# A two-layer decoder on one core: the first expert layer starts on full tiles of four sequences, and the rest of its routing runs beside them

## The reference

```
x = x + L0_attn(layernorm(x));  x = x + L0_xattn(layernorm(x), ctx, ctx, mask)
x = x + L0_ffn(layernorm(x))
x = x + L1_attn(layernorm(x));  x = x + L1_xattn(layernorm(x), ctx)
x = x + L1_ffn(layernorm(x))

def L0_ffn(x):                                   # 8 experts, 2 of them for each row
    probs = softmax(x @ router_w + router_b)
    topk_p, topk_i = top_k(probs, 2);  topk_p = topk_p / sum(topk_p)
    for e in range(8):
        w = sum(where(topk_i == e, topk_p, 0))
        out += w * (relu(x @ w1[e] + b1[e]) @ w2[e] + b2[e])
```

## Time and profile before

| what | us |
|---|---|
| device time, median of 3 runs | 2476.54 |
| the same, lowest and highest run | 2468.53 and 2481.51 |
| the profiled execution, its own time | 2488.47 |
| its span, first to last instruction | 2486.7 |

### The profile page before, as it was taken

The page is one execution under the profiler, slowest core; times in us unless marked ns, Lnnn a source line. Parts: engine busy times, 40 slices in busy tenths (PEclk is TensorE's granted clock), DMA queues, the critical chain, the costliest instruction groups (busy, mean ns, idle before and its releaser), DMA issues. The chain is left out here.

```text
span 2486.7 us, 41779 instructions
## 1 busy us (share of the span) xinstructions
PE 2199.1 (88%) x13780; PEld 1754.8 (71%) x13781; DVE 1184.5 (48%) x3431; ACT 962.1 (39%) x1878; POOL 640.5 (26%) x820
## 2 busy tenths in 40 slices
PE   6997887838999668888888969988999999999998
PEld 4664454527999545555555547778999999999998
DVE  4543788743333356666676535535422222222245
ACT  2221554413444324444444422330155555555411
POOL 1112667756000313333332211113600000000053
PEclk9997989859999768989999889989999999999999
DMA  9920000112222133333333110025401111111033
GB/s 318 386 97 1 1 1 33 51 71 81 70 70 72 61 83 82 82 73 71 77 86 70 35 54 4 4 84 189 143 29 34 34 35 34 34 34 34 26 102 104
DMA packets 150997, 183.31 MB, mean 74 GB/s; under 512 B 25491, under 2 KB 119251, under 8 KB 150739
## 3 DMA queue, kind: packets, MB, share of 16 engines
q1 hardware_dynamic: 136962, 146.51, 20.6%
q0 software_dynamic: 12288, 33.57, 4.3%
q10 hardware_dynamic: 1616, 1.57, 0.2%
HBM read 73.34 MB, written 74.19 MB: 59 GB/s over the span
## 5 line engine op out<-in xcount | busy, mean ns | idle before, releaser
L2257 ACT ACTIVATE a_prob<-a_st_ps 128x512 f32<-128x512 f32 (+1 forms) x384 | 197.7, 522 | 297.3 <-PE a_st_ps L2135 295.1
L2333 DVE CUSTOM_DVE_ANT_0 a_s_ps<-a_s_ps,a_causal 128x512 f32<-128x512 f32 (+3 forms) x512 | 241.2, 515 | 120.5 <-PE a_s_ps L2118 119.4
L1774 PE MATMUL e_up_ps<-e_xT,e_ring 128*128 128x128 f32 x2272 | 276.8, 275 | 0.0
L1774 PEld LDWEIGHTS e_up_ps<-e_xT,e_ring 128*128 128x128 f32 x2272 | 270.7, 192 | 3.6
L1726 POOL DMA_INDIRECT e_wgu<-slots_y,slot x64 | 61.1, 954 | 617.4 <-DMA slots_y<-e_y 572.7
L1804 ACT ACTIVATE e_ring<-e_wgu 128x512 f32 (+2 forms) x355 | 180.9, 531 | 76.1 <-PE e_up_ps L1774 74.4
L2118 PE MATMUL a_s_ps<-a_ks,rf_qs 68*128 68x512 f32 (+3 forms) x512 | 157.3, 375 | 58.1 <-DVE a_most L2333 44.8
L1809 ACT ACTIVATE e_hT<-e_up_ps 128x512 f32<-128x512 f32 x103 | 61.5, 597 | 369.7 <-PE e_y_ps L1784 362.3
L2135 PE MATMUL a_st_ps<-rf_qs,a_ks 128*128 128x512 f32 (+3 forms) x512 | 188.0, 418 | 13.6 <-DMA rf_qs<-a_m_lo 10.3
L2045 POOL TENSOR_SCALAR_AFFINE_SELECT a_prob<-a_prob 128x256 f32<-128x256 f32 x256 | 101.0, 419 | 369.8 <-ACT a_prob L2257 369.6
L1784 PE MATMUL e_y_ps<-e_wd,e_hT 128*128 x852 | 195.7, 380 | 0.0
(11 more groups left out here) (420 smaller groups left out, 4028.3 us busy)
## 6 DMA issues: line engine op xcount, KB each, us to landing
slots_x<-zero_row SPq DMA_DIRECT2D x4, 8448.0 KB, 50.2
e_xin<-slots_x SPq DMA_DIRECT2D x142, 128.0 KB, 2.0
slots_y<-e_y SPq DMA_DIRECT2D x142, 128.0 KB, 1.7
e_w<-in_L_ffn_w SPq DMA_DIRECT2D x16, 512.0 KB, 10.1
rf_qs<-a_hi SPq DMA_DIRECT2D x32, 256.0 KB, 5.0
a_ks<-a_hi SPq DMA_DIRECT2D x32, 256.0 KB, 5.1
rf_qs<-a_lo SPq DMA_DIRECT2D x32, 256.0 KB, 6.1
a_ks<-a_lo SPq DMA_DIRECT2D x32, 256.0 KB, 7.1
```

Of the source, the lines that this page charges most:

```text
L1774: last = pe.matmul(up_ps[:, j, bank, (first + n) * P:(first + n + 1) * P], weights, xT[:, j, k * P:(k + 1) * P], start=k == 0, stop=k == K ...
L2257: act.activation(prob[:, gr % 2, u // 3, (u % 3) * BANK:(u % 3) * BANK + cols], st_ps[:, u % 2, 0:cols], ACT.Exp).then_inc(exp_done, 1)
L2333: last = dve.tensor_tensor_reduce(s_ps[:, u % 2, off:off + cols], s_ps[:, u % 2, off:off + cols], causal[:, S - cols:], 1.0, -3.0e38, ALU. ...
```

## The change

The routing's state (rows, norm, `StreamedChoice`, semaphores) is held by a class `Routing` that lives through both stages. Cross attention ends after STEPS = (B + 1) * TB = 36 steps, with groups 0 to 2 placed and the 32 scatters of groups 0 and 1 issued, and with the logits of sequence 6 and the statistics of sequence 7 made. From the counts after groups 0 and 1 `order_first` takes 24 tiles that are full, level by level over the experts, and `words` writes the rows and words of these alone.

The expert stage has its first 28 tiles written out. Inside them stand the scatters of groups 2 to 4 (POOL, 32), the rows, transposes and logits of sequence 7, choice, count and `slots` of groups 3 and 4, the order of the other 47 tiles (`order_rest`, `place_rest`, `turn_order`, `words`), and the copy of the places. `late.gpsimd` follows POOL's scatters, `late.sync` stands at tile 9, `late.sync_slopes` at tile 23, `late.vector` at tile 20. y is stored back to the tile's own place in slots_x, and L1 attention gathers from there; `pack` is gone. DVE's order per tile becomes x, y, h; h goes straight into hT, where Relu works in place. The buffers of `late` and w_of now lie in a spare area. The core of the diff:

```
+FIRST_TILES = 24
+FIRST_WORDS = FIRST_TILES // UNROLL
...
+    def tiles_of(self, dve, tiles, over):
         self.link(dve, dve.tensor_tensor(tiles, self.base[:, :], self.first[:, :], ALU.subtract))
...
+        if over:
+            self.link(dve, dve.tensor_scalar(tiles, tiles, float(over), None, ALU.add))
+        self.link(dve, dve.tensor_copy(self.tiles_i[:, :], tiles))
+        self.link(dve, dve.tensor_scalar(self.tiles_i[:, :], self.tiles_i[:, :], P.bit_length() - 1, None, ALU.logical_shift_right))
+        self.link(dve, dve.tensor_copy(tiles, self.tiles_i[:, :]))
+    def levels(self, dve, tiles):
+        shape = [P, EXPERT_TILES, E]
+        self.link(dve, dve.tensor_tensor(self.by_level[:, :, :], tiles.unsqueeze(1).broadcast_to(shape),
+                                         self.level[:, :].unsqueeze(2).broadcast_to(shape), ALU.min))
+        self.link(dve, dve.tensor_reduce(self.reach[:, :], self.by_level[:, :, :], AX.X, ALU.add))
+    def find(self, dve, tiles, place):
+        self.link(dve, dve.tensor_scalar(self.within[:, :], self.reach[:, :], place, None, ALU.is_le))
+        self.link(dve, dve.tensor_reduce(self.depth[:, :], self.within[:, :], AX.X, ALU.add))
+        self.link(dve, dve.tensor_tensor(self.within[:, :], self.within[:, :], self.reach[:, :], ALU.mult))
+        self.link(dve, dve.tensor_reduce(self.begun[:, :], self.within[:, :], AX.X, ALU.max))
+        self.link(dve, dve.tensor_scalar(self.past[:, :], self.begun[:, :], place, -1.0, ALU.subtract, ALU.mult))
+        self.link(dve, dve.tensor_scalar(self.more[:, :], tiles, self.depth[:, 0:1], None, ALU.is_gt))
+        self.link(dve, dve.tensor_tensor_scan(self.until[:, :], self.g.ones[:, 0:E], self.more[:, :], 0.0, ALU.mult, ALU.add))
+        self.link(dve, dve.tensor_scalar(self.under[:, :], self.until[:, :], self.past[:, 0:1], None, ALU.is_le))
+    def order_first(self, dve):
+        full, gone, more = self.full[:, :], self.gone[:, :], self.more[:, :]
+        self.levels(dve, full)
+        self.find(dve, full, self.place[:, 0:1])
+        self.link(dve, dve.tensor_reduce(self.spot[:, 0:1], self.under[:, :], AX.X, ALU.add))
+        dve.scalar_tensor_tensor(out=self.spot[:, 1:2], in0=self.spot[:, 0:1], scalar=float(EXPERT_TILES), in1=self.depth[:, :],
+                                 op0=ALU.mult, op1=ALU.add).then_inc(self.ordered, 1)
+        dve.wait_ge(self.ordered, 1)
+        self.find(dve, full, float(FIRST_TILES))
+        self.link(dve, dve.tensor_tensor(more, more, self.under[:, :], ALU.mult))
+        self.link(dve, dve.tensor_scalar(gone, full, self.depth[:, 0:1], None, ALU.min))
+        self.link(dve, dve.tensor_tensor(gone, gone, more, ALU.add))
...
+    def order_rest(self, dve):
+        left, depth, spare, more = self.tiles[:, :], self.depth[:, :], self.spare[:, :], self.more[:, :]
+        self.tiles_of(dve, left, P - 1)
+        self.link(dve, dve.tensor_tensor(left, left, self.gone[:, :], ALU.subtract))
+        self.levels(dve, left)
+        self.find(dve, left, self.place[:, 0:1])
...
+    def place_rest(self, dve):
...
+    def turn_order(self, pe, part, bank):
+        pe.wait_ge(self.ordered, part + 1)
+        pe.matmul(bank[0:1, 0:P], self.spot[:, 0:1], self.g.ident[:, :], start=True, stop=True)
+        pe.matmul(bank[0:1, P:2 * P], self.spot[:, 1:2], self.g.ident[:, :], start=True, stop=True).then_inc(self.order_turned, 1)
+    def words(self, dve, part, bank):
+        at, until = ((0, FIRST_TILES), (FIRST_TILES, SLOT_TILES))[part]
+        word_at, word_until = ((0, FIRST_WORDS), (FIRST_WORDS, EXPERT_WORDS))[part]
+        dve.wait_ge(self.order_turned, part + 1)
...
+        dve.tensor_copy(self.g.tile_rows[0:1, at:until], bank[0:1, P:P + until - at]).then_inc(self.written, 1)
...
+    def keep_slots(self, dve):
         dve.wait_ge(self.placed, self.groups)
...
+        dve.tensor_copy(self.g.slot[:, :, :].rearrange("p t c -> p (t c)"), self.slot[:, :]).then_inc(self.written, 1)
...
-        STEPS = (B + 3) * TB
+        STEPS = (B + 1) * TB
...
-                ready = sum(n * TB for b, n in GROUPS if (b + n + 2) * TB + 2 < s) * 2
+                ready = sum(n * TB for b, n in GROUPS[0:2] if (b + n + 2) * TB + 2 < s) * 2
...
-            for j in range(RROWS):
-                pool.wait_ge(sorted_[j], 16 * 2 * TB * B // RROWS)
+            rnorm.gpsimd(B - 1)
+            rnorm.gpsimd_offset(B - 1)
...
+            pe.wait_ge(p_kept, NT)
+            route.turn_order(pe, 0, turn[:, 0, :])
...
                 for gr, t, n in chosen(i, 2):
+                    if i == STEPS - 2:
+                        route.tiles_of(dve, route.full[:, :], 0)
                     route.slots(dve, gr, t, n, seq_bank)
+                    if i == STEPS - 2:
+                        dve.wait_ge(g.zeroed, 16 * ZERO_PARTS)
+                        route.order_first(dve)
...
-            route.words(dve)
-            route.pack(dve)
-            dve.wait_ge(route.written, 3)
+            after(dve, rnorm.offset_done, B - 1)
+            dve.wait_ge(x_done, NT)
+            rnorm.vector_stats(B - 1)
+            keep_logits(B - 2)
+            route.words(dve, 0, turn[:, 0, :])
+            dve.wait_ge(route.written, 2)
...
+def over_tiles(eng, n, steps, first=1):
     looped = (n - UNROLL) // UNROLL
-    for i in range(UNROLL):
-        steps(i, i, 0, None)
-    with eng.Fori(1, looped) as u:
+    for i in range(first * UNROLL):
+        steps(i, i % UNROLL, i // UNROLL, None)
+    if first > 1:
+        for i in range(first * UNROLL, (first + 1) * UNROLL):
+            steps(i, i % UNROLL, i // UNROLL, None)
+        first += 1
...
+            for j in range(routing.RROWS):
+                sp.wait_ge(routing.sorted[j], 16 * 2 * TB)
             for i in range(AHEAD):
                 fetch(i, i)
-            late.sync()
-            late.sync_slopes()
...
             def steps(i, place, u, kind):
                 j = place % 2
+                if kind or 2 <= i:
+                    sp.wait_ge(y_kept, i - 1)
+                    sp.dma_start(rows_x[tile_row(i - 2)], y[:, j, :]).then_inc(y_out[j], 16)
+                if not kind and i + AHEAD == FIRST_TILES:
+                    sp.wait_ge(route.written, 4)
+                    for n in range(routing.RROWS):
+                        sp.wait_ge(routing.sorted[n], 16 * 2 * TB * B // routing.RROWS)
                 if kind or i + AHEAD < N:
                     fetch(i + AHEAD, place)
-                if kind or 2 <= i:
-                    sp.wait_ge(y_kept, i - 1)
-                    sp.dma_start(rows_y[i - 2], y[:, j, :]).then_inc(y_out[j], 16)
-            over_tiles(sp, N, steps)
+                if not kind and i == 9:
+                    sp.wait_ge(routing.l_done, B)
+                    late.sync()
+                if not kind and i == FIRST_TILES - 1:
+                    late.sync_slopes()
+            over_tiles(sp, N, steps, FIRST_WORDS)
...
+                if not kind and i in (2, 4):
+                    turn_routed(i // 2 - 1)
+                if not kind and i == 6:
+                    logit()
+                if not kind and i in (4, 11):
+                    gr = {4: 3, 11: 4}[i]
+                    route.count(pe, gr, TB, routing.before[:, :], route_bank)
+                if not kind and i == 15:
+                    route.turn_order(pe, 1, route_bank)
+            over_tiles(pe, N, steps, FIRST_WORDS)
...
-                    after(act, y_done, i - 2)
-                    act.activation(hT[:, 1 - j, :], h[:, 1 - j, :], ACT.Relu).then_inc(hT_kept, 1)
-            over_tiles(act, N, steps)
+                    act.activation(hT[:, 1 - j, :], hT[:, 1 - j, :], ACT.Relu).then_inc(hT_kept, 1)
+                if not kind and i == 0:
+                    rnorm.scalar_rows(LAST, free=[(routing.sorted[LAST % routing.RROWS], LAST // routing.RROWS * 16 * 2 * TB)], buf=LAST % routing.RROWS)
+                if not kind and i in (1, 8):
+                    gr = {1: 3, 8: 4}[i]
+                    route.exponentials(act, gr, GROUPS[gr][0] * TB, TB)
+                if not kind and i in (3, 5):
+                    keep_routed(i // 2 - 1)
...
+            for k in range(2 * TB * 4, 2 * NT):
+                t = k // 2
+                pool.wait_ge(route.placed, sum(1 for b, n in GROUPS if b * TB <= t))
+                pool.indirect_dma_start(g.slots_x, bass.IndirectOffsetOnAxis(ap=route.slot[:, k:k + 1], axis=0),
+                                        rnorm.rows[t // TB % routing.RROWS][:, t % TB, :], None).then_inc(routing.sorted[t // TB % routing.RROWS], 16)
+            for j in range(routing.RROWS):
+                pool.wait_ge(routing.sorted[j], 16 * 2 * TB * B // routing.RROWS)
             late.gpsimd(g)
...
-            late.vector()
             dve.wait_ge(biases, 32)
+            def choose(i):
+                if i in (0, 7):
+                    gr = {0: 3, 7: 4}[i]
+                    if gr == 4:
```

(34 more changed lines are left out.)

178 lines of the change are left out of this document (97 added, 81 removed).

## The result

The kernel before took 2473.69 us (median of 5 runs, 2468.53 to 2481.51), the changed one 2456.17 us (2450.13 to 2459.14). The ratio is 0.9921, with a 95% interval of 0.9902 to 0.9940: faster by 0.79%, some 19.5 us. The forecast was 2444.4 us, in a range of 2431 to 2459: the sign is right and the time lies in the range, near its upper end, but of a gain of 32 us only 18 to 20 arrived. The measured 2456 is the number that rival B had, and lies outside the 2434 to 2453 that the forecast gave itself. The changed kernel was measured again on two other chips, at 1.0019 (0.9995 to 1.0044) and 1.0016 (0.9993 to 1.0039) of the kernel before. There it gains nothing that these intervals show.

What follows compares the result with a forecast made beforehand. Before the experts the routing chain, no busy engine, sets the time; in the expert stage PE bounds. 45.2 - 6.0 - 4 - 1 - 1 - 0.9 = 32 us saved, so the median 2476.5 becomes 2444.4 us, range 2431 to 2459.

Steps and rivals of the forecast that it cites:

- rival B: Expert stage: DVE's blocks and POOL's work beside them hurt PE, costs together 25 of 45 us, total 2456; chance 0.17.
- The hole: Cross attention to first expert transpose: that transpose moves from 566.6 to 521.4, saving 45.2 us, with 1 us for the boundary.
- rival C: Boundary before the expert stage: 5.6 us of POOL's pause stay, total 2450 us; chance 0.11.
- PE's products: Expert stage: moved-in transposes 1.2, logits 2.1, counts 2.4 and turn_order 0.3 add 6.0 us on full PE.
- DVE's blocks: Expert stage: routing steps exceed 1.7 us of slack per tile by 4.7 in sum; taken as 4 us, ends 0 and 8.
- DVE beside POOL: Expert stage, words(1): five two-input DVE instructions may meet POOL's preparation, 0 to 8 us; taken as 1.
- ScalarE: Expert stage: the w1 copy behind the later Relu ends near 807.7 against 807.97, just hidden; 1 us taken for slips.
- The end: End of the expert stage: the row read of the last y store adds 0.9 us.
- The base: Whole kernel: the profiled 2488.5 us lies 12 above the median 2476.5, so 2456 becomes 2444.4.
- D: Expert stage: the wait only moves, to second words at tile 24 or SP's question at tile 20; 2477 us; chance 0.04.
- E: Expert stage: SP sets the pace, gain lost from 4.2 us per tile on; 2499 us, 23 slower; chance 0.04.
- A: Whole kernel: the forecast itself holds, 2444 us, its own range 2434 to 2453; chance 0.64.

Runs made afterwards that it cites:

- paced: The changed kernel with GpSimd waiting for each of the expert stage's 32 scatters to land before issuing the next; 2462.04 us, 0.9952 of before.
- the rest added: The changed kernel plus a block between expert stage and second attention where only GpSimd works, some 43 us; 2567.16 us, 1.0183 of before.
- the filled hole: The kernel before with 36 unused 128x512 products on TensorE in its idle stretch ahead of the experts; 1.0043 of before.
- before_inplace: The kernel before with only the expert's bias add written into hT, last of VectorE's three steps, and Relu in place; 1.0035 of before.
- scatters: The kernel before, tiles still looped, with 32 scatters of x to an unread scratch tensor behind GpSimd's preparation; ran once, 2472.99 us.

## Why the prediction was right, and which terms were not

**The hole.** The forecast had 7.8 us from logits(6) to the first transpose, it is 10.1. The instruction chain was counted well: 3.2 us from the product's end to POOL's last operation (503.95 to 507.13) against 3.8. The transpose comes 2.6 us behind POOL's first instruction, not 3.0. The failed step is the boundary: "I take the 1 us, since that boundary too has no scatter before it". It is 4.26 us, of which 2.7 are the drain, and the run with the drain moved gave 2.7 back. The boundary at 213.87 was the wrong neighbour: what counts in these traces is not whether a scatter is near, but whether the block has had any. That was rival C's mechanism with half its size, given 0.11.

**PE's products.** Forecast 6.0. By themselves they took 6.5: 1.2 for the transposes, 1.85 for the logits, 2.7 for the counts and 0.75 for *turn_order*. The five tiles that hold them (2, 4, 6, 11 and 15) are 5.5 us longer than before's.

**DVE's blocks.** Forecast 4. Tile 14, behind *order_rest*, is 2.2 us longer (forecast 2.3) and tile 10 0.5; the others were hidden: 2.7. The 3.9 us of waiting for e_xT hold 1.6 of the stage's first tiles, where before has 2.9. PE's timeline at tile 15:

```profile
575.77 1.24 PE L1576 MATMUL e_y_ps<-e_w,e_hT 128*128 x5
579.04 2.05 PE L1566 MATMUL e_h_ps<-e_xT,e_spare 128*128 128x128 f32 x16 [2.03 <-DVE e_xT L1636]
```

**DVE beside POOL.** Forecast 1, with 0 to 8 as its ends. It is at most 0.5. DVE's timeline in *words(1)*:

```profile
589.24 0.98 DVE L760 SCALAR_TENSOR_TENSOR r_word<-r_word,r_expert_f 1x13 f32<-1x13 f32 x5
590.25 0.61 DVE L761 CAST experts<-r_word 1x13 int32<-1x13 f32 x1
```

POOL's beside it:

```profile
588.50 3.22 POOL L1444 TENSOR_SCALAR rf_placed<-e_spare,rf_of_place 6x512 f32<-6x512 f32 x2
```

The five instructions with two inputs take 0.98 us, 0.20 each. The conversion behind them takes 0.61, where the same line took 0.16 in *words(0)*, and begins where the second of POOL's two does; tile 17 is 0.2 us longer for it. In the *paced* kernel GpSimd begins this preparation only at 608.74, the same conversion (591.30) takes 0.16 and tile 17 takes 3.73, so the 0.2 us are GpSimd's. The rule from the Trainium skill's "SBUF — State Buffer" ("Who interferes with whom") would have allowed 7 us by the prediction's estimate. The trace doesn't bear it out here: the five ran at their usual pace through a POOL instruction of 1.6 us that reads and writes SBUF, and the one held, for 0.45, has a single input.

**ScalarE.** Forecast 1 ("just hidden"). This is the term that was mis-sized: some 0.32 + 0.10 us at the head of each turn of the loop, 3.8 us from tile 27 to 60 and 6.7 where the in-place add stood alone, with its longer loop. (That loop, the one of before, runs over 60 tiles, 4 to 63, and not over the 56 named at the start.) The 0.87 from Relu to copy was read at tile 64, which loads a new word in the code written out behind the loop. At the head of a turn before itself had 1.09, as at tile 60 (789.57 to 790.66):

```profile
790.66 1.06 ACT L1487 ACTIVATE e_w_of<-e_w 128x1024 f32 x1 [0.46 <-issue]
```

In the changed kernel it is 1.25 to 1.33 in the loop (641.70 to 643.03 is the longest), and the 0.3 us by which the copy was to be hidden (807.7 against 807.97) were less than the 0.38 to 0.46 between them and 0.87. At the new words of the written-out tiles 8 to 24 it is 0.73, and nothing is lost.

**The end.** Forecast 0.9, measured 0.8 (from the stage's last addition of y to the next stage's first instruction, 3.39 against 2.64).

**The sum.** The stage and its boundary cost 12.8 us where the forecast had 12.9: ScalarE at 3.8 and more instead of 1, but POOL beside DVE at 0.2, DVE 1.3 less, the products 0.5 less and tiles 0, 1 and 3 together 1.2 us shorter than in before; 1.2 are spread over single tiles and the last product's end. The sum was right because its errors met. The net of the change's own stretches is 30.1 against 32.

**The base.** The number by the median, 2444.4, is 12 us short of 2456.17. At 0.45 us for a us at 0.50 (0.40 from the fit through the 17 runs of before, 0.53 through the 12 paced ones) the mean span on the first kind of chip, less 0.45 of its time at 0.50 outside the hole, is 2362.0 in before, 2332.6 in the first 5 runs of the change and 2331.9 in the 12 paced ones: 29.4 and 30.1 us less. So the change's 30 us are there, and 20 to 37 us more at 0.50 take 9 to 17 back. (Which chip the first 5 ran on is not on record.) On the second kind the same sum gives 2387.5 and 2369.8: 18 less, the stalls having eaten part, and 46 us more at 0.50 (339 against 293), some 25 of them in the stalled expert stage. What lies outside that stage the profiles put mostly in the second attention, which stood at 0.50 for 106 to 143 us in the six profiles of before's kind and for 128 to 148 in the eight of the change's. Why is open. That it was the rest lost with the hole is excluded by the rest added, and made unlikely by the filled hole; that it is the time at which the stages now begin wasn't tried.

**The rivals.** B's signs are absent: no instruction over 1 us in *words(1)*, 3.9 us of waiting for e_xT and not over 8. C is half true. D and E are excluded: PE doesn't idle at tile 24, and SP's fetches are on time, 3.73 per tile. The median of 2456 equals B's number all the same, and by another way: the change's own stretches gave A's sum, and the clock took the rest. On the second kind of chip DVE's copies do keep PE waiting, for 15.3 us, as B's price has it, but by no mechanism that B named. No rival held that the chips would differ.

## What to carry to other kernels

Work moved off an idle stretch is worth what the stretch shows, less what it costs where it goes, and one trace gave the net to 2 us, though single terms were off by up to 3; but the runs also differ by where the clock falls to 0.50, here by 15 us between one profile and its own median, so compare stretches in profiles and medians in runs, never one profile's span with another's. Before a burst of indirect DMAs is put beside other engines' work, measure on more than one chip, and let GpSimd reach the end of its block early. Read the price of a repeated step where it repeats: the row behind a loop can be cheaper than its like inside. Where a buffer is saved by working in place, look for the engine in whose order a step that now comes late stands ahead of one that must be early.

## What the hardware showed that was not expected

- Chips differ by kind. Two of three later chips ran the last expert stage in 854 to 862 us and the third, like the first measurement, in 816 to 819, with the same code. On the slow kind VectorE executed nothing for 11.5 us, and TensorE one product per 0.7 to 2.8 us, while GpSimd issued an indirect DMA every 1.27 us. A product on TensorE that waits for nothing and still comes late speaks for a lack of instructions, and against a lock between VectorE and GpSimd; no run tested it. The Trainium skill's "Runtime: NRT & Kernel Launch", section "Instruction fetch mechanics", calls the crossing of a 16 KiB boundary of code "mostly hidden". On the first kind the trace agrees: 28 tiles written out show no cost but 1.8 us of a clock that came back later. On the second no run separated code from scatters. Short bursts cost nothing even there: the second attention, with its bursts of 4 and 8 gathers, took 603.4 us in *before_inplace* and 603.5 in *scatters* on the first kind, both with 105.8 us at 0.50.
- GpSimd's drain at the end of a block: 0.07 us past its last operation, or 0.05 us long, where the block had no indirect DMA; 2.7 where the last one had ended 15 us before; 7.0 behind a burst.
- Forty us without work on any engine but GpSimd left the time at 0.50 elsewhere as it was, 346 us against 339.
